# Attention: the transposition of a step's maxima moved behind three score units of the following step

## The reference

```python
def attention(x):                       # 16 heads of 16 dimensions, 1024 tokens, 2 sequences
    q, k, v = ...                       # A: one key and value head for all query heads, with biases; B: 16 of each
    scores = q @ k.T / 4                # B adds slope[head] * (key position - query position)
    scores = where(key > query, -inf, scores)
    return softmax(scores) @ v          # then the output projection
ffn(x) = shared_expert(x) + top-2 of 8 routed experts   # gates by sigmoid scores
```

## Time and profile before

| what | value |
|---|---|
| median of 3 runs | 1035.86 us (1034.84 to 1036.69) |
| the profiled execution | 1033.63 us |
| its span | 1031.9 us |
| PE busy | 964.2 us (93%) |
| VectorE busy | 760.6 us (74%) |
| ACT busy | 570.4 us (55%) |
| POOL busy | 411.3 us (40%) |
| chain that ended last, PE's share | 71% |
| chain that ended last, VectorE's share | 16% |

### The profile page before, as it was taken

The page is one execution under the profiler, slowest core; times in us unless marked ns, Lnnn a source line. Parts: engine busy times, 40 slices in busy tenths (PEclk is TensorE's granted clock), DMA queues, the critical chain, the costliest instruction groups (busy, mean ns, idle before and its releaser), DMA issues.

```text
span 1031.9 us, 19370 instructions
## 1 busy us (share of the span) xinstructions
PE 964.2 (93%) x6370; PEld 613.2 (59%) x6370; DVE 760.6 (74%) x2132; ACT 570.4 (55%) x1078; POOL 411.3 (40%) x434
## 2 busy tenths in 40 slices
PE   4888999999889999999998989999999899999998
PEld 3433333333358889988886433333334588899887
DVE  6798999999256776447778979999992568764475
ACT  4525777777744335653354647777777533466332
POOL 3420634333435417625843102323225361374570
PEclk9879999999989999999999989999999999999999
DMA  4721212210105215733249523334401251266351
GB/s 142 193 46 30 47 44 44 44 44 9 49 26 203 80 47 173 181 122 120 67 116 218 118 36 69 61 70 77 76 13 44 84 173 53 82 190 160 117 183 48
DMA packets 66755, 95.40 MB, mean 92 GB/s; under 512 B 19669, under 2 KB 50821, under 8 KB 64599
## 3 DMA queue, kind: packets, MB, share of 16 engines
q1 hardware_dynamic: 46645, 52.74, 19.0%
q10 hardware_dynamic: 13100, 22.53, 8.6%
q0 software_dynamic: 6912, 18.88, 7.0%
HBM read 66.79 MB, written 26.67 MB: 91 GB/s over the span
## 4 chain that ended last, share of the span: by engine, by line
PE 71%; DVE 16%; issue 4%; DMA 3%; ACT 3%; POOL 2%; SPq 1%; ACTq 0%; DVEq 0%; POOLq 0%
PE o_ps L1101 13%; PE st_ps L1084 8%; PE su_ps L1043 7%; PE st_ps L293 7%; PE st_ps L294 7%; PE st_ps L295 7%; PE o_ps L1241 4%; PE st_ps L1043 4%; PE su_ps L1241 3%; DVE mab L1729 3%; PE su_ps L1147 3%; DVE unread L1725 3%; PE st_ps L1276 2%; DVE xn L1604 1%; PE su_ps L293 1%
## 5 line engine op out<-in xcount | busy, mean ns | idle before, releaser
L1446 ACT ACTIVATE pt<-st_ps 128x512 f32<-128x512 f32 (+1 forms) x584 | 312.0, 596 | 161.3 <-PE st_ps L1084 153.5
L1084 PE MATMUL st_ps<-qs,ks 99*128 99x512 bf16 (+9 forms) x768 | 211.8, 328 | 4.3 <-DMA qs<-nmx 2.4
L807 POOL TENSOR_SCALAR_AFFINE_SELECT pt<-pt 128x512 f32<-128x512 f32 x120 | 74.7, 641 | 311.7 <-ACT pt L1446 311.7
L1043 PE MATMUL su_ps<-ks,qs 102*128 102x512 bf16 (+7 forms) x538 | 155.2, 330 | 11.5 <-DVE mc L1725 4.5
L1101 PE MATMUL o_ps<-pt,vp 128*32 128x512 f32 (+3 forms) x1536 | 156.6, 505 | 0.0
L1725 DVE CUSTOM_DVE_ANT_0 unread<-su_ps,cst 128x384 f32<-128x384 f32 (+3 forms) x324 | 143.0, 479 | 16.2 <-PE su_ps L1043 15.5
L1729 DVE TENSOR_REDUCE mab<-su_ps 128x1 f32<-128x512 f32 (+2 forms) x181 | 118.6, 683 | 7.2 <-PE su_ps L1043 5.1
L1043 PEld LDWEIGHTS su_ps<-ks,qs 96*128 96x128 bf16 (+1 forms) x538 | 48.5, 98 | 122.4 <-DVE mab L1729 44.4
L888 POOL DMA_INDIRECT rows_in<-rows,source x80 | 79.1, 989 | 97.5 <-DVE source L1988 73.7
L1084 PEld LDWEIGHTS st_ps<-qs,ks 99*128 99x128 bf16 (+2 forms) x768 | 73.1, 98 | 63.5 <-ACT pt L1446 16.6
L1472 ACT CAST hh<-hf 128x512 fp32r<-128x512 f32 x64 | 39.7, 620 | 123.2 <-DVE hf L1943 123.2
(11 more groups left out here) (234 smaller groups left out, 1975.7 us busy)
## 6 DMA issues: line engine op xcount, KB each, us to landing
wu_raw<-w_units_dram SPq DMA_DIRECT2D x32, 384.0 KB, 3.2
outs<-rows_out ACTq DMA_DIRECT2D x40, 256.0 KB
q_parts<-hml SPq DMA_DIRECT2D x16, 384.0 KB, 3.1
wexp_raw<-w_units_dram SPq DMA_DIRECT2D x16, 384.0 KB, 6.5
inv<-inverses SPq DMA_DIRECT2D x128, 32.0 KB, 1.8
rows<-xn SPq DMA_DIRECT2D x8, 512.0 KB, 6.2
qs<-q_parts ACTq DMA_DIRECT2D x10, 384.0 KB
k_parts<-hml SPq DMA_DIRECT2D x8, 384.0 KB, 2.9
```

The source lines that it names most:

```text
L807: pool.affine_select(block, block, [[0, 4], [1, P]], ALU.is_ge, 0.0, base=0, channel_multiplier=-1).then_inc(masked, 1)
L1043: last = pe.matmul(out_b[:, c0:c0 + width], query_columns(s, slice(0, rows), j0 + a, P * qt, P * qt + P), key_stack(l, s)(j0 + a)[0:rows, ...
L1084: last = pe.matmul(out_b[:, at:at + hi - lo], key_stack(l, s)(j)[0:rows, P * kt:P * kt + P], query_columns(s, slice(0, rows), j, lo, hi), ...
L1446: act.activation(exponentials(S, q)[:, j, 0:width_of(s, q)], bank[KM_BANKS[i % len(KM_BANKS)]][:, 0:width_of(s, q)], ACT.Exp, scale=1 / np ...
```

## The change

For steps 2 to 6 (`turned_late`), the transposition stands behind units 0, 1 and 2 of the following step instead of before them, on PE and on VectorE, and the numbers in the ring of banks are exchanged accordingly (`unit_number`). The join of `mab` stays where it was (`join_maxima`). For these steps SP sends the maxima before it gathers the sums of part 0. In all steps the rest of the three-part split is written into the free columns of the transposition's own PSUM bank and not to SBUF, and the bank is given back after the last of the four instructions, not after the second. The lead of the units goes from 0.2 to 0.36 step, in all steps. `INVERT_AT` goes from (6, 27) to (10, 26).

```diff
--- before.py
+++ after.py
@@ -167,6 +167,23 @@
     return NSU * S - len(range(0, S, STEPS))
+def turned_late(s):
+    return 2 <= s < STEPS - 1
+def unit_number(S, u):
+    s = S % STEPS
+    if u == NSU - 1 and turned_late(s):
+        return unit_base(S) + u + UNITS_AHEAD
+    if u < UNITS_AHEAD and turned_late(s - 1):
+        return unit_base(S) + u - 1
+    return unit_base(S) + u
+UNITS_AHEAD = 3
 ADDED = [[u for u in range(len(SU)) if SU[u][5] and not by_matmul(s, u)] for s in range(STEPS)]
@@ -184,7 +201,7 @@
     at = added_turn(S, u) - 2
-    return unit_base(added_units(S)[at][0]) + added_units(S)[at][1] + 1 if at >= 0 else 0
+    return unit_number(*added_units(S)[at]) + 1 if at >= 0 else 0
 def units_behind_pieces(l, lead):
@@ -194,6 +211,8 @@
     at = np.concatenate([s + np.cumsum(w) / w.sum() for s, w in enumerate(work)])
     cost = np.array([share * width + P for _, _, _, share, width, _ in SU] + [4 * CH], float)
     through = np.cumsum(cost) / cost.sum()
+    passed = np.cumsum(np.insert(cost[:-1], UNITS_AHEAD, cost[-1])) / cost.sum()
+    passed = np.append(np.delete(passed, UNITS_AHEAD), 1.0)
     behind = [[] for _ in at]
     left = range(BEFORE_PIECES[l], len(SU))
     for i, u in enumerate(left):
@@ -208,10 +227,14 @@
             n += 1
         behind[n].append((1, u))
     for s in range(2, STEPS):
-        for u, t in enumerate(s - 1 - lead + through):
+        for u in range(NSU):
+            t = s - 1 - lead + (passed[u] if turned_late(s - 1) else through[u])
             while at[n] < t - 1e-9 or u > 1 and n < FIRST_PIECES - 1:
                 n += 1
-            behind[n].append((s, u))
+            if u < NSU - 1 or not turned_late(s):
+                behind[n].append((s, u))
+            if u == UNITS_AHEAD - 1 and turned_late(s - 1):
+                behind[n].append((s - 1, NSU - 1))
     return behind
@@ -219,12 +242,12 @@
 SECOND_AT = (HALF_PIECES - 1, 7)
 SECOND_BY = 0.98
 AHEAD = (8, 8)
-UNITS_BEHIND = [units_behind_pieces(l, 0.2) for l in range(2)]
+UNITS_BEHIND = [units_behind_pieces(l, 0.36) for l in range(2)]
 FC_BEHIND = {10 + 3 * t: t for t in range(QT)}
 PV_LAG = 2
 PV_BEHIND = 1
-INVERT_AT, DIVIDE_BEHIND = (6, 27), (2, 4)
+INVERT_AT, DIVIDE_BEHIND = (10, 26), (2, 4)
 QKV = [[("kv", 0), ("q", 0), ("q", 1)],
        [("q", 0), ("q", 1), ("k", 0), ("k", 1), ("v", 0), ("v", 1)]]
...
@@ -634,7 +656,7 @@
             def send_half(l, half):
-                sp.wait_ge(nm_done, maxima_count(l, 0, half))
+                sp.wait_ge(half_taken, 2 * l + half + 1)
                 for part in range(3):
                     row = ROWS + l * ALIBI + part
                     sp.dma_start(first_queries(slice(row, row + 1), half),
@@ -643,7 +665,7 @@
             def send_maxima(l, s):
                 r, S = s % SBANKS, step_no(l, s)
-                sp.wait_ge(nm_done, maxima_count(l, s, 0))
+                sp.wait_ge(su_used, unit_number(S, NSU - 1) + 1)
                 for part in range(3):
                     row = ROWS + l * ALIBI + part
                     sp.dma_start(qs[row:row + 1, r, :, :], nmx[:, S % 2, part, :]).then_inc(max_in[r], 16)
@@ -705,10 +727,12 @@
                         load_unit(l, 1)
                     if s:
                         spread_inverses(S - 1, 1)
+                    if turned_late(s + 1):
+                        send_maxima(l, s + 1)
                     gather_sums(S, 0)
                     if s == STEPS - 2:
                         load_unit(l, 0)
-                    if s + 1 < STEPS:
+                    if s + 1 < STEPS and not turned_late(s + 1):
                         send_maxima(l, s + 1)
                     if l == 0 and s == 0:
                         sp.wait_ge(w_split, 4)
...
@@ -1062,7 +1086,7 @@
             def transpose_maxima(l, s):
                 S = step_no(l, s)
-                n = unit_base(S) + NSU - 1
+                n = unit_number(S, NSU - 1)
                 pe.wait_ge(mc_done, S + 1)
                 pe.wait_ge(su_used, n - len(SU_BANKS) + 1)
                 pe.transpose(bank[SU_BANKS[n % len(SU_BANKS)]][0:32, 0:P], mc[:, S % 2, :, :].rearrange("p j t -> p (j t)"), ident).then_inc(su_ready, 1)
@@ -1709,7 +1733,7 @@
             def maximum(l, s, u):
                 qt, half, j0, share, width, diagonal = SU[u]
                 S = step_no(l, s)
-                n = unit_base(S) + u
+                n = unit_number(S, u)
                 dve.wait_ge(su_ready, n + 1)
                 if s == 0 and qt < HALF:
                     to = mab[:, 1, 0, j0:j0 + share, qt]
@@ -1728,16 +1752,17 @@
                 else:
                     dve.tensor_reduce(to, src.rearrange("p (j k) -> p j k", j=share), AX.X, ALU.max).then_inc(su_used, 1)
-            def negative_parts(src, rows, a, taken, count, done):
+            def negative_parts(turned, rows, a, taken, count, done):
+                src, rest = turned[:, 0:P], turned[:, P:2 * P]
                 dve.tensor_scalar(nmx[rows, a, 0, :], src, -1.0, None, ALU.mult).then_inc(nm_step, 1)
-                dve.wait_ge(nm_step, 2 * done - 1)
-                dve.scalar_tensor_tensor(nmr[rows, :], src, -1.0, nmx[rows, a, 0, :], ALU.mult, ALU.subtract).then_inc(taken, 1)
-                dve.wait_ge(taken, count)
-                dve.tensor_copy(nmx[rows, a, 1, :], nmr[rows, :]).then_inc(nm_step, 1)
-                dve.wait_ge(nm_step, 2 * done)
-                dve.tensor_tensor(nmx[rows, a, 2, :], nmr[rows, :], nmx[rows, a, 1, :], ALU.subtract).then_inc(nm_done, 1)
+                dve.wait_ge(nm_step, 3 * done - 2)
+                dve.scalar_tensor_tensor(rest, src, -1.0, nmx[rows, a, 0, :], ALU.mult, ALU.subtract).then_inc(nm_step, 1)
+                dve.wait_ge(nm_step, 3 * done - 1)
+                dve.tensor_copy(nmx[rows, a, 1, :], rest).then_inc(nm_step, 1)
+                dve.wait_ge(nm_step, 3 * done)
+                dve.tensor_tensor(nmx[rows, a, 2, :], rest, nmx[rows, a, 1, :], ALU.subtract).then_inc(taken, 1)
             def half_parts(l, half):
@@ -1747,17 +1772,22 @@
                     dve.tensor_tensor(mab[:, 1, 1, :, :], mab[:, 0, 0, :, :], mab[:, 0, 1, :, :], ALU.max).then_inc(mc_done, 1)
                     maximum(l, 1, 0)
                 dve.wait_ge(turned_half, 2 * l + half + 1)
-                negative_parts(bank[4 + half][0:16, 0:P], slice(0, 16), half, half_taken, 2 * l + half + 1, maxima_count(l, 0, half))
+                negative_parts(bank[4 + half][0:16, 0:2 * P], slice(0, 16), half, half_taken, 2 * l + half + 1, maxima_count(l, 0, half))
+            def join_maxima(l, s):
+                S = step_no(l, s)
+                a = S % 2
+                dve.wait_ge(su_used, unit_base(S) + NSU - 1)
+                dve.tensor_tensor(mc[:, a, :, HALF:QT], mab[:, a, 0, :, :], mab[:, a, 1, :, :], ALU.max).then_inc(mc_done, 1)
             def maxima_parts(l, s):
                 S = step_no(l, s)
-                n = unit_base(S) + NSU - 1
+                n = unit_number(S, NSU - 1)
                 a = S % 2
-                dve.wait_ge(su_used, n)
-                dve.tensor_tensor(mc[:, a, :, HALF:QT], mab[:, a, 0, :, :], mab[:, a, 1, :, :], ALU.max).then_inc(mc_done, 1)
                 dve.wait_ge(su_ready, n + 1)
-                negative_parts(bank[SU_BANKS[n % len(SU_BANKS)]][0:32, 0:P], slice(0, 32), a, su_used, n + 1, maxima_count(l, s, 0))
+                negative_parts(bank[SU_BANKS[n % len(SU_BANKS)]][0:32, 0:2 * P], slice(0, 32), a, su_used, n + 1, maxima_count(l, s, 0))
             def invert(S, part):
                 dve.wait_ge(sums_in, 16 * (2 * S + part + 1))
@@ -1786,8 +1816,12 @@
                             for part in range(2):
                                 if s and u == INVERT_AT[part]:
                                     invert(step_no(l, s - 1), part)
+                            if u == UNITS_AHEAD and turned_late(s):
+                                maxima_parts(l, s)
                             maximum(l, s + 1, u)
-                        maxima_parts(l, s + 1)
+                        join_maxima(l, s + 1)
+                        if not turned_late(s + 1):
+                            maxima_parts(l, s + 1)
                 invert(step_no(l, STEPS - 2), 0)
                 invert(step_no(l, STEPS - 2), 1)
```

5 lines of the change are left out of this document (2 added, 3 removed).

## The result

The change makes the kernel slower: 1046.33 us median (1044.68 to 1047.12), against 1035.35 of the kernel before in the same comparison, a ratio of 1.0106 [1.0084, 1.0128]. The profiled execution has a span of 1045.1 us. The prediction had 1030.9.

A forecast was written before the change was run, and what follows sets the result against it. PE and VectorE, limiting each other by turns, were taken to bound the step, not DMA. Handshake -7.5, last transpositions -0.5 and lead +3.0 gave -5.0 us: median 1030.9, range 1024 to 1038.

The forecast's parts named there:

- The handshake: Ten middle-step boundaries of the attention layers: the moved transposition saves 0.75 us a step, -7.5 us, bounds -24 and +8.
- both PE waits: At each boundary, PE's waits for the join and for a bank, 0.51 us each, 1.02 together, would go.
- PE has four pieces and values without a unit: While VectorE splits at the boundary, PE has about 1.9 us of other work, covering its second wait.
- VectorE's side: At each boundary VectorE is freed of 0.38 us transposition wait and 0.26 us net in the split, 0.64 in all.
- near the VectorE side: The 0.75 us a step, taken between VectorE's freed 0.64 and PE's 1.02.
- The reciprocals: Before units 10 and 26: VectorE waits 0.2 us for part 0's sums at the median; part 1's arrive just in time.
- Rival C: VectorE waits at reciprocals for late sums, 1.2 us in each of ten steps: 1043, or 1038 with 0.7; chance 0.17.
- The clock of the burst: The longer burst at each layer's start can add a low-clock stretch: +0.2 us a layer, bounds -1.2 to +1.7.
- The middle of layer 0: First piece of step 1 to last transposition: five pieces and seven units fewer, -4.1 us; -8.1 with the other gains.
- The tail: After the last transposition, per layer: five pieces without units, +2.7 us; step 7 no longer waits for maxima, -1.2.

The follow-up runs named there:

- e5: The kernel before with lead 0.36 in place of 0.2 and the reciprocals before units 13 and 32: 1039.2 us, ratio 1.0044.
- e2: The kernel after with the reciprocal of part 1 before unit 32 and not 26: 1038.11 us, ratio 1.0038.
- f1: The kernel before with lead 0.36 in the middle only and reciprocals before units 13 and 32: 1035.2 us, ratio 0.9994.
- e7: The kernel after with lead 0.36 in the middle only, step 7's maxima ahead of the sums, part 1's reciprocal before unit 32: 1030.76 us, ratio 0.9957.
- e6: The kernel before with only the split's rests in PSUM and the bank held to the split's end: 1033.87 us, ratio 0.9988.
- e4: The kernel after with one more 512-column matmul ahead of each of units 1 to 14 of the burst: 1040.45 us, ratio 1.0056.
- e3: The kernel after with SP sending step 7's maxima ahead of the sums too: 1043.13 us, ratio 1.0076.
- f3: The kernel after with lead 0.2 and the reciprocals before units 10 and 32: 1080.77 us, ratio 1.0456.

## Why the prediction was wrong

**The handshake: right in kind, 0.42 us a step and not 0.75.** "I take both PE waits as gone" held in the middle of layer 0: no wait of PE for VectorE is left there. But a step that loses 2 x 0.51 us of PE's waits should be 26.8 us long, and it is 27.37. What failed here is that nothing was looked for behind the waits: "PE has four pieces and values without a unit" was counted as cover for VectorE, while the same four pieces run into ACT, which costs 0.42 us a step. The remaining 0.2 is not accounted for. That ACT's pace costs this is read from the timeline; no run removed it. How much of the 0.42 us is the late transposition's and not the lead's stays open: by e5 against e2 it is worth 0.25 of 0.37 us a step (with the rest in PSUM), by f1 against e7 0.10 of 0.33.

**VectorE's side.** 0.38 + 0.26 us were freed as said (the split: 0.60 to 0.28, the cast 0.21 to 0.28). The 0.26 us were worth nothing by themselves: e6 has a step of exactly 27.79 us. The forecast lay "near the VectorE side" of two freed times, when it was PE's waits that counted. The Trainium skill, "SBUF — State Buffer", section "Who interferes with whom", names the conflict that e6 removes; the trace agrees in duration, 0.60 against 0.28 us, and the time of the kernel hardly moved.

**The reciprocals: the largest loss, and the step of the prediction that failed.** "651.3, against 650.8 by the slowest landing. Just in time." Two things in this reckoning were wrong. The landing of "1.4 to 3.2 us, median 2.1" is not that of the sums. Of the copies that touch `sums`, the trace tells such a time only for the one that writes the inverses out (L659), here for the whole run:

```profile
DMA to landing us min/median/max: 1.4/1.8/3.2
```

The sums' own copy (L654) takes 1.9 us for part 0 in all middle steps of the kernel before, but for part 1 in layer 1 it takes 5.14 us in the first step and 3.8 to 4.2 in the next four, by its last semaphore update. The sums issued at 647.57 were there at 651.6, behind the 651.3. And the reckoning was made for a middle step, where unit 26 stands behind piece 13. In step 1 of a layer it stands behind piece 10, seven pieces ahead of where unit 27 was, not four. So VectorE came to the reciprocal 8.7 us behind the first piece and not 13.2, 4.5 us earlier; 1.5 us had been spare, and 3.0 were waited. The window from issue to landing, before and after, shows busy DMA engines in both (0.64 and 0.72):

```profile
619.81:624.95 5.14, 5.08 (x36) 1.80 (x29) 5.10 (x15) 3.73 (x8) 1.23 (x2) 1.00 0.64 121
```

```profile
627.07:632.14 5.07, 2.45 (x18) 0.77 (x10) 1.71 (x3) 2.54 (x5) 1.22 (x2) 1.00 0.72 123
```

That the loads beside it make this copy slow is likely, and no run tested it. The cost is shown by e2: 8.2 us. Part 0, whose sums land in 1.9 us in the middle steps, waited nowhere in them. Rival C had the mechanism ("in layer 1 the one of part 1, whose landing runs beside the loads") and the wrong form: one wait of 3 us and one of 1.0, not 1.2 us in each of ten steps, and behind the first 6.8 us at half clock, which no part of the prediction had priced.

**The clock of the burst: +0.2 us a layer taken, and it held in layer 1 only.** The bursts grew by 4.5 and 4.2 us, against +4.1 with the clock in it. In layer 0 the lower clock now also covers the 2.39 us behind the burst, 1.2 us of loss that were not there before. In layer 1 the kernel before had this already: values of 2.79 us at 610.46 and about 2 us behind its burst at half clock (1.55 after).

```profile
610.46 2.79 PE L1101 MATMUL o_ps<-pt,vp 128*32 128x256 f32 x16
```

So what filling gives back (e4) is not an error of the prediction by its size: a part of it is a cost that the kernel before has too.

**The middle of layer 0: -3.8 and not -8.1** (5 x 0.75, 0.25 for the last transposition and 4.1 for the work moved out). 5 x 0.33 = 1.65 of the missing 4.3 are the handshake, 1.2 the half clock behind the burst by its rows (e4, without it, has a middle only 0.5 us shorter), and 1.0 the last transposition, which directly behind unit 37 waits 1.35 us for its join and not 0.35. The order of the instructions showed that place, and the prediction passed over it. 0.45 is not accounted for.

**The tail: +2.7 held, -1.2 did not come.** "SP sends them behind the sums of piece 27 and they land close to piece 35" says what happened, and then counts it as nearly free. From SP's issue at 267.93 three DMAs take 1.84 us, and the last lands about 2 us later, at 271.8. e3 takes this away: 3.2 us by the medians, 2.1 of them in the two tails.

**The sum.** Predicted -5.0, measured +11.0 by the medians. In the profiled executions the stretches of the table add up to +12.6, that is 17.6 from the forecast: 4.3 in the middle of layer 0, 10.3 in that of layer 1, 2.5 in the tails and 0.5 in the bursts. By cause, from the rows, the two waits for sums with the clock behind the first are 3.3 + 3.0 + 0.9 = 7.3 (rounded), the handshake 10 x 0.33 = 3.3, SP's order 2.5, the last transpositions 2 x 1.0, the half clock behind layer 0's burst 1.2 and the bursts 0.5. That is 16.8; 0.8 is not accounted for. That the range missed too comes from treating the corrections as small, when all of them went the same way.

## What to carry to other kernels

A wait that goes leaves the time of the next in line: before a freed wait is counted, lay out the same stretch for the third engine too, here four pieces in a row against ACT's pace. When work is moved ahead of a transfer that VectorE waits for in order, work out the spare time at every place where that happens, from that transfer's own landing and not from a neighbour's, and add the clock that PE loses while it stands still. A lead belongs where it is needed: the late transposition can't do without it in the middle steps (f3). At the two ends it costs: with it in the middle only, e7 has a burst of 8.99 us and tails of 30.29, against 11.94 to 12.15 in e2 and 32.93 in e3, for a middle that is 3.5 to 4.3 us longer than e2's.
